# A graph layer and 64 routed experts on one core: the beginning in another order

## The chip, the core and the metric

The kernel runs on one core of a Trainium2 chip. The metric is the device time of one execution in microseconds (us). TensorE multiplies, VectorE, ScalarE and GpSimd compute elementwise, and SyncE only issues DMAs in the kernel before. Each engine works through its own program in order, and semaphores tie them together.

## The reference, cut to what matters

```python
# x: 1024 nodes x 512;  16384 edges (src, dst, edge_weight), sorted by dst
def gnn(H, W, bias, edge_row, edge_col, edge_val):
    HW = H @ W
    msgs = edge_val[:, None] * HW[edge_col]
    out = segment_sum(msgs, edge_row, num_segments=1024)
    return relu(out + bias)

x = x + gnn(layernorm(x), W, bias, src, dst, edge_weight)
# 64 experts, 2 per token, hidden 256, plus one small shared expert
n = layernorm(x)
x = x + sum over the token's two experts e of w_e * ffn_e(layernorm(n)) + shared(layernorm(n))
```

The change lies wholly in the first part: the weighted adjacency matrix A (1024 x 1024, built from the edge list) and HW = layernorm(x) @ W. What follows (messages A @ HW, routing, experts) is computed as before.

## The kernel before, in words

**Adjacency.** The 16384 edges make 128 tiles of 128 edges. For a tile, ScalarE builds a one-hot matrix `osl` (line 587, eight tiles at a time, then one Relu at line 590), and VectorE and GpSimd build weighted one-hots `M` (lines 835 and 459; the buffers are named `M` and `AT` in rows, since two of four lie in the tile AT). Four tiles are a quad. TensorE multiplies them into one of four PSUM banks (line 1129), and VectorE adds that bank into A (`sums`, lines 803 to 812: clear the bank that was added before, line 811; add, line 812). The program has 32 quads. VectorE's adds run three quads behind its `M` tiles (`BEHIND`). In each quad GpSimd makes one `M` tile and VectorE three. `osl` has two buffers, each for two quads, so ScalarE may build the next only when TensorE has used the buffer.

**x.** The rows of x are 8 blocks of 128. A block's way is: mean and variance (VectorE, lines 736 to 745), inverse deviation (GpSimd, line 430), the standardised rows `xh` (VectorE, line 821), four transposes (TensorE, line 1117), a copy to `xhT` (ScalarE, line 594), the product with W (TensorE, line 1136), a copy to HW (ScalarE, line 599). In the rows fp32 matmuls are counted twice: a quad is 8 of them, a product is 8.

**The order.** TensorE goes through four pairs of blocks (`pair`). For each block it does: transposes of the block, four quads, the product. In what follows *a block* is this unit: four quads with one block of x. At the start come the edge arithmetic on VectorE (lines 749 to 797), which ends in `edges_ready`, and transposes of small weights on TensorE (lines 1097 and 1105, `raw`). SyncE issues all loads, the last being x blocks 2 to 7 and W (lines 306 and 307), then a fill of the DRAM tensor `slots` (`sentinel`), then the weights of the first four expert pairs. ScalarE clears all of A (line 579). GpSimd scales the small shared weights (lines 470 and 471: `R` and `Wsb`) after its first pair.

After the last product TensorE waits for all adds (line 1148), transposes A (line 1156) and goes on with the messages.

Of the kernel before, what the change touches and what calls it, by code (L numbers as in the profile page):

```python
# [21 lines left out]
POOL_M = 1  # L22
# [13 lines left out]
def moe_gnn(nc, x, src, dst, ew, W, bias, Wg, bg, gamma, beta, W1, b1, W3, b3, W2, b2,  # L36
# [18 lines left out]
    with ctx:  # L55
# [58 lines left out]
        sentinel = HW[:, 0:5, :].rearrange("p b d -> p (b d)")[:, 0:(EXPERTS * LIST + P) * REC // P]  # L114
# [172 lines left out]
        def _(sp):  # L287
# [5 lines left out]
            v3 = "e (c d) -> e c d"  # L293
            for to, a in ((raw_wg, Wg), (raw_g, gamma), (raw_b, beta)):
                sp.dma_start(to, a.rearrange(v3, c=4)).then_inc(raw_in, 16)
            sp.dma_start(raw_b13[:, 0:2, :], b1.rearrange(v3, c=HC)).then_inc(raw_in, 16)
            sp.dma_start(raw_b13[:, 2:4, :], b3.rearrange(v3, c=HC)).then_inc(raw_in, 16)
            sp.dma_start(gs4[:, 0, :], gs.rearrange("(p c) -> p c", c=DC)).then_inc(small_in, 16)
            sp.dma_start(gs4[:, 1, :], bs.rearrange("(p c) -> p c", c=DC)).then_inc(small_in, 16)
# [3 lines left out]
            sp.dma_start(Ws[:, :, 0:32], Ws1.rearrange("(p c) n -> p c n", c=DC)).then_inc(ws_in, 16)  # L303
            sp.dma_start(Ws[:, :, 32:64], Ws3.rearrange("(p c) n -> p c n", c=DC)).then_inc(ws_in, 16)
            for i in range(1, 4):
                sp.dma_start(X[:, 2 * i:2 * i + 2, :], xv[:, 2 * i:2 * i + 2, :]).then_inc(x_in[i], 16)
            sp.dma_start(GW[:, :, :], W.rearrange("(p c) n -> p c n", c=DC)).then_inc(gw_in, 16)

            sp.wait_ge(consts, 6)
# [12 lines left out]
            for v in range(RING // 2):  # L322
                load_up(v, v)
                load_down(v, v)
# [81 lines left out]
        def _(pool):  # L406
# [10 lines left out]
            g.memset(sentinel, NOWHERE).then_inc(consts, 1)  # L417
# [4 lines left out]
                   allow_small_or_imprecise_dtypes=True).then_inc(consts, 1)  # L422
            pool_n = [0]
# [13 lines left out]
            inverse_deviations(range(0, 2), 1)  # L437
            pool.wait_ge(edges_ready, 1)
            R1 = pool.value_load(rounds_sb[0:1, 0:1], min_val=1, max_val=N // WIN)

            def pair(r, j, first):

                half = (r * (NB // 2) + j) * 4
                for h in range(4):
# [6 lines left out]
                    for q in (2 * h, 2 * h + 1):  # L451
                        if not first or q >= 4:
                            pool.wait_ge(quad_done[q % 2], half + (q // 2 - 1))
                        elif q == 2:
                            pool.wait_ge(raw_transposed, 2)
                        hold(pool)
                        for k in range(POOL_M):
# [6 lines left out]
            inverse_deviations(range(2, NB), 2)  # L464

            pool.wait_ge(small_in, 80)
            pool.wait_ge(ws_in, 32)
            pool.wait_ge(raw_transposed, 2)
            for c in range(DC):
                g.tensor_scalar(R[:, c, 64:128], Ws[:, c, :], gs4[:, 0, c:c + 1], None, ALU.mult)  # L470
                ins = g.tensor_scalar(Wsb[:, c, :], Ws[:, c, :], gs4[:, 1, c:c + 1], None, ALU.mult)
            ins.then_inc(wsb_ready, 1)
# [104 lines left out]
        def _(act):  # L577
            a = nc.scalar
            a.memzero(A[:, :]).then_inc(a_chain, 4)
# [12 lines left out]
            def x_transposed(g, u):  # L592
                act.wait_ge(xhT_ps, g + 1)
                a.copy(xhT[:, u, :, :].rearrange("p c n -> p (c n)"), bank[4 + u][:, :]).then_inc(xhT_ready, 1)

            def x_times_w(g, u):
                act.wait_ge(hw_ps, g + 1)
                act.wait_ge(sentinel_out, 16)
# [789 lines left out]
```

## Time and profile before

| | |
|---|---|
| times of three runs | 458.48, 459.57, 460.67 us; median 459.57 |
| the profiled execution | 458.82 us, its span 457.1 us |
| TensorE busy | 391.7 us (86%) |
| VectorE, ScalarE, GpSimd busy | 207.7, 166.1, 154.9 us |
| moved by DMA | 126.11 MB, 276 GB/s on average |

The first fifth of the span (to 85.5 us) is the part with A and HW; from there to about 160 us come the messages and the routing, then a short serial part, and from about 190 us the experts. The chain of waits ends with TensorE for 81% of the span.

### The profile page before, as it was taken

Reading aid. Unit: us, or ns where it says so; the run is one execution under the profiler, and the core shown is the slowest. Engines: PE = TensorE matmul, PEld = TensorE weight load, DVE = VectorE, ACT = ScalarE, POOL = GpSimd, SP = SyncE. Lnnn points to the kernel's source line nnn. Section 1 sums busy time; section 2 is a strip of 40 time slices with the busy share of each in tenths; the row PEclk is TensorE's granted clock in tenths of the full one; section 3 lists DMA queues with packets and bytes.
Section 4 is the critical chain, followed back from the end, with each engine's and each line's share of the span. In section 5 each row is a group of like instructions: output and inputs, shape, how many; then the busy total and the mean of one; then the engine's idle time right before and its main releaser. Section 6 shows DMA issues by size and latency. Waiting matters only on the chain.

```text
span 457.1 us, 6545 instructions
## 1 busy us (share of the span) xinstructions
PE 391.7 (86%) x1811; PEld 202.3 (44%) x1812; DVE 207.7 (45%) x685; ACT 166.1 (36%) x414; POOL 154.9 (34%) x262
## 2 busy tenths in 40 slices
PE   2699999999999987999999999986988979888600
PEld 1586767656565553344344443433434433343100
DVE  5889888216666586532333233313113123222036
ACT  9859999223223220233233323331213231131200
POOL 2575553014654657232333223323113122110000
PEclk9989999999999995899999999999889898898855
DMA  4999600100004545499999999999999999996068
GB/s 113 328 383 408 276 0 0 42 25 24 24 25 122 222 156 197 144 389 408 404 408 407 405 408 409 407 406 408 407 406 409 406 405 404 403 405 271 20 250 303
DMA packets 41779, 126.11 MB, mean 276 GB/s; under 512 B 7953, under 2 KB 8529, under 8 KB 41618
## 3 DMA queue, kind: packets, MB, share of 16 engines
q1 hardware_dynamic: 35954, 117.29, 66.3%
q0 software_dynamic: 5792, 8.43, 5.3%
q8 instruction: 14, 0.23, 0.2%
q14 instruction: 19, 0.16, 0.1%
HBM read 121.22 MB, written 13.39 MB: 294 GB/s over the span
## 4 chain that ended last, share of the span: by engine, by line
PE 81%; issue 5%; DMA 5%; DVE 3%; SPq 3%; POOL 1%; ACT 1%; ACTq 0%; DVEq 0%; POOLq 0%
PE bank L1295 29%; PE bank L1312 13%; PE bank L1168 12%; PE bank L1129 6%; PE bank L1136 6%; PE bank L1304 5%; PE bank L1288 4%; DMA w<-totals 2%; DMA X<-in_x_dram 2%; PE bank L1156 2%; PE bank L1187 1%; PE bank L1236 1%; PE bank L1177 1%; PE bank L1117 1%; SPq L398 1%
## 5 line engine op out<-in xcount | busy, mean ns | idle before, releaser
L1031 DVE SCALAR_TENSOR_TENSOR osl<-bank,b13T,osl 128x64 f32<-128x64 f32 x132 | 28.4, 277 | 171.5 <-ACT osl L675 171.5
L1295 PE MATMUL bank<-w,xhT 128*64 128x512 f32 x368 | 91.9, 645 | 14.7 <-issue 14.5
L668 ACT COPY xh<-bank 128x512 f32<-128x512 f32 x33 | 19.3, 585 | 149.0 <-PE bank L1295 149.0
L1168 PE MATMUL bank<-HW,AT 128*128 128x512 f32 x128 | 58.2, 592 | 0.0
L1295 PEld LDWEIGHTS bank<-w,xhT 128*64 128x64 f32 x368 | 28.6, 147 | 61.5 <-issue 60.1
L545 POOL DMA_INDIRECT totals<-osl,A x17 | 17.0, 1000 | 91.5 <-PE bank L1288 72.1
L1312 PE MATMUL bank<-w,osl 128*64 128x512 f32 x184 | 45.0, 608 | 3.2 <-DVE osl L1031 3.2
L545 POOL DMA_INDIRECT totals<-GW,A x16 | 16.0, 999 | 87.2 <-PE bank L1288 71.6
L587 ACT ACTIVATE osl<-iota,eT 128x128 f32<-128x128 f32 x128 | 39.0, 389 | 6.1 <-PE bank L1129 6.1
L541 POOL DMA_INDIRECT A<-nx_rows,A x33 | 34.4, 1041 | 10.5 <-issue 10.5
L1168 PEld LDWEIGHTS bank<-HW,AT 128*128 128x128 f32 x128 | 22.9, 191 | 21.0 <-issue 21.0
L675 ACT ACTIVATE osl<-bank,b13T 128x64 f32<-128x64 f32 x132 | 30.7, 314 | 4.0 <-issue 1.0
L1304 PEld LDWEIGHTS bank<-ident,xh 128*128 128x128 f32 x132 | 18.3, 208 | 26.6 <-issue 26.0
L1136 PE MATMUL bank<-GW,xhT 128*128 128x512 f32 x64 | 28.8, 592 | 0.0
L1312 PEld LDWEIGHTS bank<-w,osl 128*64 128x64 f32 x184 | 14.5, 140 | 28.6 <-issue 28.6
L1304 PE MATMUL bank<-ident,xh 128*128 128x128 f32 x132 | 24.6, 309 | 0.5 <-ACT xh L668 0.5
L1129 PE MATMUL bank<-AT,osl 128*128 128x128 f32 x128 | 19.3, 302 | 4.6 <-DVE AT L835 3.7
L1014 DVE TENSOR_TENSOR xhT<-xhT,bT 128x512 f32<-128x512 f32 x32 | 22.2, 692 | 1.1
L1288 PE MATMUL bank<-ident,A 128*128 128x128 f32 x132 | 22.3, 293 | 0.0
L1295 PE MATMUL bank<-A,xhT 128*64 128x512 f32 x80 | 20.0, 644 | 2.3 <-issue 2.3
L1013 DVE TENSOR_TENSOR xhT<-bank,gT 128x512 f32<-128x512 f32 x32 | 21.8, 681 | 0.2 <-issue 0.2
L1295 PE MATMUL bank<-HW,xhT 128*64 128x512 f32 x80 | 20.0, 644 | 2.0 <-issue 1.9
(208 smaller groups left out, 543.2 us busy)
## 6 DMA issues: line engine op xcount, KB each, us to landing
w<-in_L_ffn_W_dram SPq DMA_DIRECT2D x66, 1024.0 KB
A<-in_L_ffn_W_dram SPq DMA_DIRECT2D x15, 1024.0 KB
HW<-in_L_ffn_W_dram SPq DMA_DIRECT2D x10, 1024.0 KB
AT<-in_L_ffn_W_dram SPq DMA_DIRECT2D x5, 1024.0 KB
w<-totals SPq DMA_DIRECT2D x8, 512.0 KB, 7.5
w<-in_L_ffn_W_dram SPq DMA_DIRECT2D x6, 512.0 KB
X<-in_x_dram SPq DMA_DIRECT2D x4, 512.0 KB, 7.2
out_dram<-X SPq DMA_DIRECT2D x8, 256.0 KB, 5.7
```

The source lines that it names most:

```text
L541: g.indirect_dma_start(xg[b], None, nx_rows, bass.IndirectOffsetOnAxis(ap=index, axis=0), bounds_check=N - 1, oob_is_err=False).then_inc(x ...
L545: g.indirect_dma_start(totals, bass.IndirectOffsetOnAxis(ap=index, axis=0), ysb[b], None, bounds_check=2 * N - 1, oob_is_err=False).then_i ...
L587: ins = a.activation(osl[:, h % 2, k, :], iota[:, :], ACT.Abs, bias=eT[:, 1, ds(j * 32 + 8 * h + k, 1)])
L675: ins = a.activation(sl[b][:, m, CAP * h:CAP * h + CAP], bank[4][:, m * P + CAP * h:m * P + CAP * h + CAP], ACT.Silu, bias=b13T[:, 0, m, c ...
L1031: ins = v.scalar_tensor_tensor(hT[b][:, m, CAP * h:CAP * h + CAP], bank[4][:, (HC + m) * P + CAP * h:(HC + m) * P + CAP * h + CAP], b13T[: ...
L1129: ins = t.matmul(bank[q % 4][:, ds(at[k], TW)], osl[:, (q // 2) % 2, (q % 2) * QUAD + k, :], Mq[q % 4][:, k, :], start=False, stop=(k == Q ...
L1136: ins = t.matmul(bank[6 + u][:, :], xhT[:, u, c, :], GW[:, c, :], start=(c == 0), stop=(c == DC - 1))
L1168: ins = t.matmul(bank[4 + s % 2][:, :], AT[:, s % 2, k, :], HW[:, k, :], start=(k == 0), stop=(k == NB - 1))
L1288: ins = t.transpose(bank[b][:, c * P:(c + 1) * P], xg[i][:, c:c + DC * (P - 1) + 1:DC], ident[:, :])
L1295: ins = t.matmul(bank[2 + b][CAP * h:CAP * h + CAP, :], xe[b][:, c, CAP * h:CAP * h + CAP], up_w[v][:, h, :, c, :], start=(c == 0), stop=( ...
L1304: ins = t.transpose(bank[4][:, i * P:(i + 1) * P], hraw[b][:, at:at + HC * (P - 1) + 1:HC], ident[:, :])
L1312: ins = t.matmul(bank[6 + b][CAP * h:CAP * h + CAP, :], hT[b][:, m, CAP * h:CAP * h + CAP], down_w[v][:, h, m, :], start=(m == 0), stop=(m ...
```

## The change

Loads: after the edge arrays and x blocks 0 and 1, SyncE now issues W and the other x blocks. The small weights are issued from ScalarE's queue ahead of everything else on it. A is cleared in three parts: columns 0 to 2599 by VectorE, to 5399 by GpSimd, the other 2920 by ScalarE. The `sentinel` values lie in an expert weight buffer instead of HW, and SyncE waits for their transfer before it loads the fourth pair's weights.

Order: a block's product now stands ahead of its quads, and the transposes of the next block stand between the two. VectorE standardises block 0 in the middle of the edge arithmetic and copies `xhT` (ScalarE copies the first one only). The statistics of x blocks 2 to 7 stand in three parts between the quads of the second block. GpSimd makes two `M` tiles in each odd quad, except in the first four quads, and scales the shared weights ahead of its first tile. ScalarE waits for that (`wsb_ready`) ahead of its second group of one-hots.

```diff
+A_DVE, A_POOL = 2600, 5400
+def pool_tiles(q, first):
+    return 2 if q % 2 and not (first and q < 4) else 1
 # sync
             sp.dma_start(X[:, 0:2, :], xv[:, 0:2, :]).then_inc(x_in[0], 16)
+            sp.dma_start(GW[:, :, :], W.rearrange("(p c) n -> p c n", c=DC)).then_inc(gw_in, 16)
+            for i in range(1, 4):
+                sp.dma_start(X[:, 2 * i:2 * i + 2, :], xv[:, 2 * i:2 * i + 2, :]).then_inc(x_in[i], 16)
...
             for v in range(RING // 2):
+                if v == RING // 2 - 1:
+                    sp.wait_ge(sentinel_out, 16)
                 load_up(v, v)
 # gpsimd
+            g.memset(A[:, A_DVE:A_POOL], 0.0).then_inc(a_chain, 1)
+            g.memset(sentinel, NOWHERE).then_inc(consts, 1)
             inverse_deviations(range(0, 2), 1)
+            pool.wait_ge(ws_in, 64)
+            pool.wait_ge(raw_transposed, 2)
+            for c in range(DC):
+                g.tensor_scalar(R[:, c, 64:128], Ws[:, c, :], gs4[:, 0, c:c + 1], None, ALU.mult)
+                ins = g.tensor_scalar(Wsb[:, c, :], Ws[:, c, :], gs4[:, 1, c:c + 1], None, ALU.mult)
+            ins.then_inc(wsb_ready, 1)
...
+                        if first and q in (5, 7):
+                            b = q - 3
+                            inverse_deviations(range(b, b + 2), b // 2 + 1)
 # scalar
-            a.memzero(A[:, :]).then_inc(a_chain, 4)
+            for to, of in ((raw_wg, Wg), (raw_g, gamma), (raw_b, beta)):
+                act.dma_start(to, of.rearrange(v3, c=4)).then_inc(raw_in, 16)
... six more loads
+            a.memzero(A[:, A_POOL:]).then_inc(a_chain, 1)
-            def pair(j, last):
+            def pair(j, first, last):
                 half = j * 4
-                x_transposed(j * 2, 0)
-                one_hots(half, j, 2, False)
-                one_hots(half, j, 3, False)
-                x_times_w(j * 2, 0)
-                x_transposed(j * 2 + 1, 1)
+                for u in range(2):
+                    if u:
+                        one_hots(half, j, 2, False)
+                    one_hots(half, j, 2 * u + 1, first)
+                    x_times_w(j * 2 + u, u)
                 if not last:
                     one_hots(half + 4, j + 1, 0, False)
-                    one_hots(half + 4, j + 1, 1, False)
-                    x_times_w(j * 2 + 1, 1)
 # vector
+            v.memset(A[:, 0:A_DVE], 0.0).then_inc(a_chain, 2)
...
+            def transposed_rows(b, u):
+                dve.wait_ge(xhT_ps, b + 1)
+                if not isinstance(b, int) or b > 1:
+                    dve.wait_ge(hw_ps, b - 1)
+                v.tensor_copy(xhT[:, u, :, :]..., bank[4 + u][:, :]).then_inc(xhT_ready, 1)
... in sum_pair, for each q
+                    if with_x and q % 4 == 3 and not (last and u):
+                        transposed_rows(b + 1, 1 - u)
+                    if with_x and first and q in (3, 4, 6):
+                        c = {3: 2, 4: 4, 6: 6}[q]
+                        mean_and_variance(range(c, c + 2))
+                    if with_x and first and q in (5, 6):
+                        dve.wait_ge(rstd_ready, 2)
+                        standard_rows(q - 3, q - 5)
+                    if with_x and not first and not last and q % 4 == 1:
+                        dve.wait_ge(rstd_ready, 4)
+                        dve.wait_ge(xhT_ps, b + 1)
+                        standard_rows(b + 2, u)
 # tensor
                 for u in range(2):
-                    if with_x:
-                        ... (transposes of this block)
+                    if with_x and not (first and u == 0):
+                        x_product(j * 2 + u, u)
+                        if not (last and u):
+                            x_rows(j * 2 + u + 1, 1 - u)
                     for q in range(4 * u, 4 * u + 4):
...
-                    if with_x:
-                        ... (product of this block)
```

On TensorE, the program from the product for the edge table to the first quad before (line 1117 is a block's transposes, the first M rows a quad):

```order
L1090 MATMUL bank<-wrow,ones 128x128
L1097 MATMUL bank<-ident,AT 128x64 x12
L1105 MATMUL bank<-ident,AT 128x64 x4
L1108 TENSOR_LOAD rounds_sb
L1108 ISA x2
L1139 UNCONDITIONAL_BRANCH
L1139 ISA
L1117 MATMUL bank<-ident,xh 128x128 x4
```

The same stretch now (line 1139 is transposes, line 1149 a product with W, line 1154 the product for the edge table, line 1172 the first quad's offsets):

```order
L1125 MATMUL bank<-ident,AT 128x64 x12
L1133 MATMUL bank<-ident,AT 128x64 x4
L1139 MATMUL bank<-ident,xh 128x128 x4
L1154 MATMUL bank<-wrow,ones 128x128
L1149 MATMUL bank<-GW,xhT 128x512 x4
L1139 MATMUL bank<-ident,xh 128x128 x4
L1159 TENSOR_LOAD rounds_sb
L1159 ISA x2
L1172 TENSOR_LOAD wrow
```

The small weights, the transposes of blocks 0 and 1 and the first product now stand ahead of the first quad.

On VectorE, the first quads' tiles before (line 821 is `xh`, 835 the `M` tiles, 741 and 744 the statistics of six x blocks, 812 the first add):

```order
L821 TENSOR_SCALAR xh<-X,mv,rstd 128x512
L826 MEMSET bank 128x384 x2
L835 TENSOR_SCALAR M<-iota,eT 128x128 x3
L821 TENSOR_SCALAR xh<-X,mv,rstd 128x512
L835 TENSOR_SCALAR M<-iota,eT 128x128 x3
L741 BN_STATS stats<-X 128x6 x6
L744 BN_AGGR mv<-stats 128x2 x6
L830 MEMSET bank 128x384 x2
L835 TENSOR_SCALAR AT<-iota,eT 128x128 x6
```

And now, from the same tiles to the tiles of the second block's second quad (line 854 `M` tiles, 828 an add, 835 the copy to `xhT`, 748 and 751 statistics of two x blocks):

```order
L854 TENSOR_SCALAR M<-iota,eT 128x128 x6
L849 MEMSET bank 128x384 x2
L854 TENSOR_SCALAR AT<-iota,eT 128x128 x6
...
L828 TENSOR_TENSOR A<-A,bank 128x384
L835 COPY xhT<-bank 128x512
L748 BN_STATS stats<-X 128x6 x2
L751 BN_AGGR mv<-stats 128x2 x2
L854 TENSOR_SCALAR M<-iota,eT 128x128 x3
...
L828 TENSOR_TENSOR A<-A,bank 128x384
L748 BN_STATS stats<-X 128x6 x2
L751 BN_AGGR mv<-stats 128x2 x2
```

The statistics have moved from between the first block's tiles to between the second block's, in three parts.

## Rows read from the trace of the kernel before

**Rows 1.** Busy time by stretch, in us from the span's start.

```profile
core 0: us, PE busy (x) PEld busy (x) DVE busy (x) ACT busy (x) POOL busy (x), PEclk, DMA share, GB/s
22.66:26.10 3.44, 3.44 (x16) 3.44 (x17) 3.36 (x12) 0.03 (x1) 0.83 (x1) 0.50 0.99 314
37.71:85.50 47.79, 46.88 (x263) 33.77 (x262) 38.80 (x117) 41.33 (x105) 20.07 (x38) 1.00 0.34 135
85.50:160.00 74.50, 74.50 (x306) 43.89 (x305) 38.62 (x169) 21.25 (x43) 34.51 (x85) 1.00 0.22 74
191.00:411.00 220.00, 202.95 (x962) 86.63 (x960) 65.86 (x188) 63.67 (x184) 59.17 (x58) 0.96 1.03 406
```

**Rows 2.** Chain of waits, the beginning: start, duration (us), what.

```profile
10.30 7.58 DMA X<-in_x_dram
...
22.66 3.67 PE bank L1129 x16
26.33 3.44 PE bank L1136 x8
...
30.23 3.57 PE bank L1129 x32
```

**Rows 3.** Chain of waits, a block and the end of the part.

```profile
62.19 2.73 PE bank L1129 x24
64.96 1.15 PE bank L1129 x8
...
69.55 0.47 PE bank L1117 x4
...
85.50 0.88 PE bank L1156 x8
```

**Rows 4.** Timeline of the beginning: start, duration, engine, line, what.

```profile
2.07 7.14 ACT L579 ACTIVATE A<-A 128x8320 uint32<-128x8320 uint32 x1
...
9.12 2.43 ACT L587 ACTIVATE osl<-iota,eT 128x128 f32<-128x128 f32 x8
...
11.54 0.29 DVE L797 TENSOR_TENSOR eT<-eT,bank 128x128 f32<-128x128 f32 x1 [0.20 <-PE bank L1090]
...
12.78 0.57 DVE L821 TENSOR_SCALAR xh<-X,mv,rstd 128x512 f32<-128x512 f32 x1 [0.94 <-DVE eT L797]
...
15.22 3.78 PE L1129 MATMUL bank<-M,osl 128*128 128x128 f32 x16 [0.64 <-POOL M L459]
...
16.54 3.94 DVE L741 BATCH_NORM_STATS2 stats<-X 128x6 f32<-128x512 f32 x6 [0.39 <-DMA X<-in_x_dram]
...
21.80 1.44 DVE L835 TENSOR_SCALAR AT<-iota,eT 128x128 f32<-128x128 f32 x6
```

**Rows 5.** SyncE's issue of a small load, from the timeline.

```profile
2.64 0.57 SPq L295 DMA_DIRECT2D AT<-in_L_ffn_Wg_dram  x1
```

**Rows 6.** DMA issues: count, KB each, median us to landing.

```profile
GW<-in_L_gnn_W_dram SPq DMA_DIRECT2D x1, 1024.0 KB, 10.0
...
HW<-in_L_ffn_Ws_dram SPq DMA_DIRECT2D x2, 64.0 KB, 5.7
```

**Rows 7.** Timeline of ScalarE and TensorE in the repeating blocks.

```profile
38.09 1.06 ACT L590 ACTIVATE osl<-osl 128x1024 f32<-128x1024 f32 x1
...
39.52 0.59 ACT L594 COPY xhT<-bank 128x512 f32<-128x512 f32 x1
...
39.97 2.35 PE L1129 MATMUL bank<-AT,osl 128*128 128x128 f32 x16 [0.47 <-POOL M L459]
...
48.18 2.45 ACT L587 ACTIVATE osl<-iota,eT 128x128 f32<-128x128 f32 x8 [0.26 <-PE bank L1129]
```

**Rows 8.** Timeline of VectorE: a copy out of PSUM, then adds in the repeating blocks.

```profile
8.02 0.54 DVE L767 COPY eT<-bank 128x384 f32<-128x384 f32 x1
...
39.16 0.38 DVE L811 MEMSET bank<- 128x384 f32 x1
...
40.84 0.38 DVE L811 MEMSET bank<- 128x384 f32 x1
```

**Rows 9.** GpSimd, its instructions of one line: duration in ns, lowest, median, highest.

```profile
L459 POOL TENSOR_SCALAR AT<-iota,small x12: 790/793/1124, 35.6 to 74.5; 128x128 f32<-128x128 f32 x12
...
L470 POOL TENSOR_SCALAR R<-HW,gs x4: 437/439/541, 29.2 to 31.8; 128x64 f32<-128x64 f32 x4
```

**Rows 10.** Timeline of VectorE: the last add into A.

```profile
82.76 0.54 DVE L812 TENSOR_TENSOR A<-A,bank 128x384 f32 x1
```

More of the change, by code:

```diff
@@ L832, in sum_pair @@
                         dve.wait_ge(raw_transposed, 2)
-                    for k in range(POOL_M, QUAD):
+                    for k in range(pool_tiles(q, with_x and first), QUAD):
                         t = j * 32 + (QUAD * q + k)
@@ L837, in sum_pair @@
                     ins.then_inc(m_ready, 1)
-                    if with_x and first and q == 1:
-                        mean_and_variance(range(2, NB))
                     if q >= BEHIND:
@@ L1088, in _ @@
             t.matmul(bank[1][0:1, P:2 * P], mx, ident[:, :], start=True, stop=True).then_inc(edges_transposed, 1)
-            pe.wait_ge(base_ready, 1)
-            t.matmul(bank[1][:, 384:512], ones[0:1, :], neg_base, start=True, stop=True).then_inc(base_ps, 1)
             pe.wait_ge(raw_in, 80)
@@ L1106, in _, with x_rows, x_product, pair @@
             ins.then_inc(raw_transposed, 1)
+            def x_rows(g, u):
+                pe.wait_ge(xh_ready, g + 1)
+                for c in range(DC):
+                    ins = t.transpose(bank[4 + u][:, c * P:(c + 1) * P], xh[:, u, c:c + DC * (P - 1) + 1:DC], ident[:, :])
+                ins.then_inc(xhT_ps, 1)
+            def x_product(g, u):
+                pe.wait_ge(gw_in, 16)
+                pe.wait_ge(xhT_ready, g + 1)
+                if not isinstance(g, int) or g > 1:
+                    pe.wait_ge(hw_ready, g - 1)
+                for c in range(DC):
+                    ins = t.matmul(bank[6 + u][:, :], xhT[:, u, c, :], GW[:, c, :], start=(c == 0), stop=(c == DC - 1))
+                ins.then_inc(hw_ps, 1)
+            x_rows(0, 0)
+            pe.wait_ge(base_ready, 1)
+            t.matmul(bank[1][:, 384:512], ones[0:1, :], neg_base, start=True, stop=True).then_inc(base_ps, 1)
+            x_product(0, 0)
+            x_rows(1, 1)
             pe.wait_ge(edges_ready, 1)
             R1 = pe.value_load(rounds_sb[0:1, 0:1], min_val=1, max_val=N // WIN)
-            def pair(r, j, with_x):
+            def pair(r, j, with_x, first=False, last=False):
                 half = pe.snap((r * (NB // 2) + j) * 4)
@@ L1131, in pair @@
                         ins.then_inc(quad_done[q % 2], 1)
-                    if with_x:
-                        pe.wait_ge(gw_in, 16)
-                        pe.wait_ge(xhT_ready, j * 2 + u + 1)
-                        for c in range(DC):
-                            ins = t.matmul(bank[6 + u][:, :], xhT[:, u, c, :], GW[:, c, :], start=(c == 0), stop=(c == DC - 1))
-                        ins.then_inc(hw_ps, 1)
-            with pe.Fori(0, NB // 2) as j:
+            pair(0, 0, True, first=True)
+            with pe.Fori(1, NB // 2 - 1) as j:
                 pair(0, j, True)
+            pair(0, NB // 2 - 1, True, last=True)
             with pe.If(R1 > 1):
```

87 lines of the change are left out of this document (36 added, 51 removed).

## The prediction

> **What bounds the kernel now.** I read the busy time by stretch first, then the chain of waits, then the timeline where the chain leaves TensorE. By stretch [rows 1] TensorE is busy for 46.88 of the 47.79 us from 37.71 to 85.50, and for all of the 74.5 us behind it. So what this part saves should move the end, if nothing later absorbs it. The experts run from 191 with the DMA at 406 GB/s, its share at the top: they are paced by loads. But each of these loads waits for a product of the experts' own (`h_ps`), so the stream of loads begins earlier when the experts do. I therefore carry a gain at 85.5 to the end in full. The chain at the beginning [rows 2] runs through the load of x that lands at 17.88, then the late start of TensorE's second half block at 22.66. The timeline [rows 4] tells why: VectorE does the statistics of six x blocks from 16.54 to 20.48 ahead of the tiles `AT` at 21.80, so TensorE, done at 19.00, stands still for 3.66 us. In the repeating blocks the chain is TensorE's alone [rows 3], but its pace is not free: three quads take 2.73 us (0.91 each) and the last 1.15.
>
> The pace tells a second thing. The first 16 quad matmuls took 3.78 us, the next 16 took 3.67, and later 32 took 3.57 [rows 2, 4]. For the second sixteen the granted clock was 0.50, the lower level of 1.2 GHz [rows 1]; the first sixteen had the same pace. TensorE had stood still before, and once it had worked for 3.4 us the product behind it went at full pace (3.44 us, as everywhere). The Trainium skill's page "TensorE: Matmul & The Clock Gate", Part 1, says that the throttled clock is the default and that work releases it; the trace agrees by those two paces. A start with less standing still saves twice, but a first product placed earlier can fall into the slow stretch.
>
> **Part 1, the beginning.** I compare the moment at which TensorE has done the quads and products of two blocks and the transposes of the third: before, 30.23 + 3.57 + 3.44 + 0.47 = 37.71 [rows 2, 3].
>
> The edge table was ready at 11.83 [rows 4]. VectorE's standardised rows of block 0 now stand ahead of it: +0.57, so 12.4; with 0.1 for crowded loads 12.5. ScalarE first issues nine loads; at SyncE's 0.57 to 0.6 each [rows 5] that is 5.4 us from 0.8, then its table (1.3 us, the stretch to 2.07 before) and 2920/8320 of 7.14 = 2.5 us of clearing: free at 10.0 instead of 9.21. Its one-hots end at 12.45 and the copy of the transposed block 0 at 13.0. The product can start at 13.1. W was 10.0 us in landing behind everything else [rows 6]; issued at 2.6 it is here by 12.6 even at that, so it costs nothing. TensorE has had only short work till then, so I take the slow clock for 3.4 us: that does 1.7 of the product's 3.44, the rest takes 1.7, then 0.47 for transposes: 18.7, and the first quad runs 19.0 to 19.9.
>
> VectorE meanwhile has made tiles of all four quads (12.5, then 0.95 as from 11.83 to 12.78, rows 0.57, two clearings 0.76, tiles 1.44, clearings 0.76, tiles 1.44: 18.4), so it no longer delays block 0. From the first quad's end it is the bound. It adds (20.0 to 20.6); copies the transposed block 1 (0.54 for 384 columns [rows 8], so 0.7 for 512: 21.3); and then does block 1's quads. A quad with three tiles takes 40.84 - 39.16 = 1.68 [rows 8]; one with two takes 0.24 less (1.44 for six tiles [rows 4]) = 1.44. Statistics for two x blocks: 3.94 for six plus the aggregates, 1.5 for two. So: statistics 22.8, quad 4 24.5, statistics 26.0, quad 5 27.4, rows of block 2 28.0, quad 6 29.7, statistics 31.2, rows of block 3 31.8, tiles and cleared bank of quad 7 32.7, its add of quad 4 and the copy of block 2 33.9. TensorE's product of block 1 and quads hide under this; quad 7 ends at 33.6. The compared moment comes at 33.8: a gain of 3.9.
>
> What hides the statistics is thus gone in block 1: 4.5 us of them, 1.4 of copies and 1.1 of rows lie on the path there, instead of one stall and a cold clock in block 0.
>
> **Part 2, the repeating blocks.** Six remain, with five sets of transposes before as now: before, (47.79 + 0.47)/6 = 8.04 us each. TensorE's own work is 3.57 + 3.44 + 0.47 = 7.48. ScalarE loses two copies of 0.59 per pair [rows 7], but it cannot run ahead: a one-hot buffer is free only when its two quads are done. From a block's quads at 0: the first buffer is free at 1.82, ScalarE starts 0.15 later, and two groups take 2 x (2.45 + 1.06) less small overlaps = 6.97 [rows 7], so the second group for the next block is ready at 8.94, or 8.94 - P after that block's quads begin, for a period P. TensorE needs another 0.82 from there to its first matmul (38.09 + 1.06 = 39.15 to 39.97 [rows 7]) and then runs the two quads in 2.1 to 2.3. So P = (9.76 - P) + 2.1 + 3.91, P = 7.88. The stretch takes 6 x 7.88 - 0.47 = 46.8 instead of 47.8, a gain of 1.0, and quads end at 80.6. Its bounds are 7.48 and 8.04 a block. VectorE per block has 2 x 1.68 + 2 x 1.44 + 0.57 + 0.7 + waits 0.2 = 7.7, GpSimd 6 tiles of 0.79 and its small copies, about 6 [rows 9]: both just fit.
>
> **Part 3, the end of the part.** Before, VectorE's last adds lay under the last product: quads ended at 82.06, the last add at 83.30 [rows 10]. That cover is gone, since quads now come last. So TensorE waits 1.24 us plus 0.15 to wake: A's transposes start at 82.0 instead of 85.50 [rows 3]. Of that part the bounds are 1.1 (one clearing and add) and 2.2 (two quads' adds behind).
>
> **At nothing.** VectorE's 2600 columns at 0.38 per 384 [rows 8] are 2.6 us, before the edge arrays are used; GpSimd's clearing and sentinel end some 2 us before it is needed. If either overran, at most 1 us. The wait for the sentinel holds only loads not used for 190 us. Earlier expert weights change nothing. GpSimd's eight scalings, 8 x 0.44 = 3.5 [rows 9], need the shared weights: issued by 5.6 and 5.7 in landing they are there at 11.3, so GpSimd is free at 14.8, in time for tiles wanted at 19.
>
> The sum: 3.9 + 1.0 - 1.4 = 3.5, which is 85.50 - 82.0. The profiled execution took 458.82, so 455.3; it lay 0.75 under the median of the runs. From the median, 459.57 - 3.5 = 456.1. I say 456.0.
>
> The Trainium skill speaks against one half of the edit: "DMA: Bandwidth & Descriptors", section "Issuing engines are not separate DMA queues", says loads issued from two engines run on the same 16 DMA engines and only issue time is saved. By it W and x land earlier because they are issued earlier and not because there are two queues. No row before shows two queues at once; the sum above goes by the order of issue alone.
>
> **The rivals.**
>
> *Clock low for longer.* If the first product goes wholly at the lower clock (+1.7), or TensorE's gaps in block 1 (2 us before the transposes of block 2, 1 before quad 7) bring the clock down again (half of 3.4 us: +1.7), the gain is 1.8, or 0.1 with both: 457.8 to 459.5. For it: the stop of 3.66 us before did it [rows 1]. Against: these stops are shorter.
>
> *Small loads late.* If the shared weights take W's 10.0 us instead of 5.7 [rows 6], they are there at 15.6, GpSimd is free at 19.1, ScalarE's second one-hots end at 22.6, and the third quad starts at 23.4 instead of 20.8. VectorE's own chain hangs on the first quad, which GpSimd's tile delays by 0.8 to 1.5. Time 457.5.
>
> *Better than summed.* If the clock is up before the first product (-1.7) and blocks take 7.6 (-1.7), the gain is 6.9: 452.7. For it: these are the lower bounds of both terms. Against: the same slow pace at 15.22 after four us of small transposes.
>
> *VectorE becomes the bound: slower.* Its 7.7 us per block rests on instructions that overlap. GpSimd gets 12 tiles a pair instead of 8. If tiles of the two hold each other up, as the highest 1124 ns of a tile at 793 suggests [rows 9], each of a block's 16 tiles could cost 0.1 more and the copy wait besides: 9.3. It decides from 7.88 + (3.5 + 2.3)/6 = 8.85 on; at 9.2 the six blocks cost 8 us more than forecast and the time is 464. Against: VectorE is idle for 9.0 of 47.79 us [rows 1], and only 0.2 us a block is added net (6.24 + 0.57 + 0.7 for 4 x 1.68 + 0.57). The Trainium skill's page "SBUF — State Buffer", "Who interferes with whom", says a VectorE instruction in a two-port mode and GpSimd lock each other out wholly. By that rule this rival gains; no row here separates it.
>
> **How the numbers follow.** Forecast 0.45 (its own range 454.7 to 457.3), clock low 0.25, small loads late 0.1, better 0.13, VectorE bound 0.07. The measurement tells a change from none at about 0.5%, or 2.3 us. Faster: nearly all of the forecast, the better case, a fifth of the two small-gain cases: 0.62. Slower 0.07, same 0.31. Range 452.8 to 459.2: it leaves out the rival on the slow side and part of the double clock loss and of the better case.
>
> **What would show it.** First quad near 19; statistics between 21 and 31 on the chain; no wait for the x load; blocks of 7.9 us; TensorE idle 1.4 us before A's transposes at about 82; the experts as long as before. A first quad after 21, blocks over 8, or a GpSimd tile on the chain would make it wrong.

## The result and the profile after

The kernel became slower: 464.5 us (median of 4 runs, 462.49 to 466.38) against 459.02 (458.41 to 460.67) for the kernel before on the same chip. The ratio is 1.012, with a 95% interval of 1.0084 to 1.0157. The forecast was 456.0. The profiled execution took 463.57 us, its span 461.8.

First the busy time by stretch of the changed kernel (columns as in [rows 1]), for the first quads, the six repeating blocks, the stretch from A's transposes on, and the experts:

```profile
core 0: us, PE busy (x) PEld busy (x) DVE busy (x) ACT busy (x) POOL busy (x), PEclk, DMA share, GB/s
25.06:28.43 3.37, 3.37 (x16) 3.37 (x17) 0.73 (x2) 2.69 (x6) 3.03 (x8) 0.50 1.03 412
41.25:88.80 47.55, 45.90 (x261) 33.29 (x259) 41.63 (x120) 41.30 (x106) 33.29 (x58) 1.00 0.17 68
90.46:164.96 74.50, 74.50 (x305) 43.98 (x306) 38.61 (x169) 20.76 (x42) 34.39 (x85) 1.00 0.22 74
195.96:415.96 220.00, 203.31 (x962) 86.89 (x960) 65.80 (x188) 63.73 (x184) 59.17 (x58) 0.96 1.03 406
```

The last two rows are those of before within 0.5 us [rows 1]. From A's transposes to the span's end it is 371.3 us, before 371.6. So the whole loss lies ahead of A's transposes, which begin at 90.46 instead of 85.50, and nothing behind them absorbs or adds anything.

The chain of waits, beginning (start, duration, what):

```profile
3.32 7.74 DMA AT<-in_L_ffn_b_dram
...
21.20 0.48 POOL R L442
...
24.12 0.82 POOL M L467
25.06 2.09 PE bank L1179 x8
```

The reader is to see two names that the chain of before had not [rows 2]: a load of small weights at the start, and GpSimd's scalings (`R`, lines 442 and 443) ahead of the first `M` tile. TensorE's timeline of the same stretch:

```profile
11.11 1.73 PE L1125 MATMUL bank<-ident,AT 64*128 64x64 f32 x12 [2.84 <-DMA AT<-in_L_ffn_b_dram]
...
14.30 0.79 PE L1154 MATMUL bank<-wrow,ones 1*128 1x128 f32 x2
15.14 6.57 PE L1149 MATMUL bank<-GW,xhT 128*128 128x512 f32 x8
21.55 0.63 PE L1139 MATMUL bank<-ident,xh 128*128 128x128 f32 x4
25.06 3.78 PE L1179 MATMUL bank<-M,osl 128*128 128x128 f32 x16 [2.88 <-POOL M L467]
```

And what the other engines waited for (GpSimd, ScalarE, VectorE):

```profile
20.20 0.55 POOL L442 TENSOR_SCALAR R<-HW,gs 128x64 f32<-128x64 f32 x1 [9.36 <-DMA gs<-in_L_ffn_bs_dram]
...
14.41 0.58 ACT L621 COPY xhT<-bank 128x512 f32<-128x512 f32 x1
...
23.77 2.44 ACT L596 ACTIVATE osl<-iota,eT 128x128 f32<-128x128 f32 x8 [6.74 <-POOL AT L443]
...
15.23 0.29 DVE L813 TENSOR_TENSOR eT<-eT,bank 128x128 f32<-128x128 f32 x1 [1.53 <-PE bank L1154]
...
27.70 0.56 DVE L828 TENSOR_TENSOR A<-A,bank 128x384 f32 x1 [6.24 <-PE bank L1179]
```

GpSimd stood still for 9.36 us until a load of 2 KB was there; ScalarE waited behind it for 6.74, then TensorE and VectorE. The row at 14.41 is the copy of the transposed block 0, which the first product reads. The loads themselves (KB each, median us from issue to landing):

```profile
AT<-in_L_ffn_b_dram ACTq DMA_DIRECT2D x2, 64.0 KB, 6.8
HW<-in_L_ffn_Ws_dram ACTq DMA_DIRECT2D x2, 64.0 KB, 10.1
...
gs<-in_L_ffn_gs_dram ACTq DMA_DIRECT2D x1, 2.0 KB, 10.1
gs<-in_L_ffn_bs_dram ACTq DMA_DIRECT2D x1, 2.0 KB, 12.9
```

The last 2 KB were issued at 7.21 and landed 12.9 us later, at 20.1. W itself took 8.5, less than the 10.0 of before [rows 6].

The end of the part is as forecast in kind:

```profile
90.46 1.13 PE L1201 MATMUL bank<-ident,A 128*128 128x128 f32 x8 [1.43 <-DVE A L828]
```

### The profile page after: what moved, and what is told of

Read it like the earlier page. It is cut to its first block, busy times and chain, and to the rows that moved or that the text cites. A ratio compares the mean times of both kernels' runs of the same rounds, so it can differ in the third digit from the quotient of the medians.

```text
span 461.8 us, 6407 instructions
## 1 busy us (share of the span) xinstructions
PE 395.0 (86%) x1811; PEld 203.6 (44%) x1812; DVE 210.3 (46%) x679; ACT 158.0 (34%) x407; POOL 170.0 (37%) x281
## 4 chain that ended last, share of the span: by engine, by line
PE 73%; issue 9%; DVE 7%; DMA 5%; DVEq 1%; POOL 1%; ACTq 1%; ACT 1%; SPq 1%; POOLq 0%
PE bank L1340 28%; PE bank L1357 13%; PE bank L1213 12%; PE bank L1349 5%; PE bank L1333 4%; DMA w<-totals 2%; PE bank L1179 2%; PE bank L1149 2%; DMA AT<-in_L_ffn_b_dram 2%; DVE A L828 2%; PE bank L1201 2%; PE bank L1232 1%; PE bank L1281 1%; DVE bank L827 1%; PE bank L1222 1%
## 5 line engine op out<-in xcount | busy, mean ns | idle before, releaser
L596 ACT ACTIVATE osl<-iota,eT 128x128 f32<-128x128 f32 x120 | 36.6, 387 | 13.5 <-POOL AT L443 6.7
L1149 PE MATMUL bank<-GW,xhT 128*128 128x512 f32 x64 | 31.9, 645 | 0.0
L467 POOL TENSOR_SCALAR M<-iota,small 128x128 f32<-128x128 f32 x23 | 19.0, 834 | 8.8 <-PE bank L1179 7.6
L1333 PE MATMUL bank<-ident,A 128*128 128x128 f32 x132 | 22.2, 293 | 0.0
```

What stands on the lines that cost most here:

```text
L596: ins = a.activation(osl[:, h % 2, k, :], iota[:, :], ACT.Abs, bias=eT[:, 1, ds(j * 32 + 8 * h + k, 1)])
L1149: ins = t.matmul(bank[6 + u][:, :], xhT[:, u, c, :], GW[:, c, :], start=(c == 0), stop=(c == DC - 1))
L1333: ins = t.transpose(bank[b][:, c * P:(c + 1) * P], xg[i][:, c:c + DC * (P - 1) + 1:DC], ident[:, :])
```

## The experiments

Times are compared with the kernel before on the same chip. That kernel's median was 458.37 us beside e1 to e4, 459.15 beside e5 to e8 and 459.45 beside e9 and e10. A difference in us is a difference of ratios times 459. Beside it stands where A's transposes begin in the profiled execution (before 85.50, changed kernel 90.46).

| kernel | median us | ratio (95%) | A's transposes |
|---|---|---|---|
| changed kernel | 464.5 | 1.012 (1.0084 to 1.0157) | 90.46 |
| e1 scalings back | 461.05 | 1.0045 (1.0024 to 1.0066) | 87.14 |
| e2 shared weights issued first | 462.69 | 1.0097 (1.0067 to 1.0126) | 88.12 |
| e3 last product last | 466.27 | 1.0182 (1.0159 to 1.0204) | 90.96 |
| e4 before + loads, clearing | 460.92 | 1.0063 (1.0042 to 1.0085) | 86.68 |
| e5 four one-hot buffers | 459.56 | 1.0001 (0.9973 to 1.0029) | 86.53 |
| e6 before + four buffers | 457.33 | 0.9950 (0.9921 to 0.9978) | 83.58 |
| e7 one queue, e1, e5 | 455.89 | 0.9931 (0.9907 to 0.9955) | 81.78 |
| e8 e7 + last product last | 456.22 | 0.9948 (0.9923 to 0.9972) | 84.01 |
| e9 e7 with two buffers | 458.19 | 0.9983 (0.9956 to 1.0011) | 83.27 |
| e10 e7, scalings first | 454.47 | 0.9886 (0.9849 to 0.9924) | 82.86 |

### The scalings back behind the first pair

```diff
 # gpsimd, ahead of its first tile
-            pool.wait_ge(ws_in, 64)
-            ... (eight scalings)
+                        elif q == 2:
+                            pool.wait_ge(raw_transposed, 2)
...
             pair(0, 0, True)
+            pool.wait_ge(ws_in, 64)
+            ... (eight scalings)
 # scalar: the wait for wsb_ready moves from its first pair to its last copy of HW
```

> The changed kernel, with GpSimd's eight scalings of the shared weights put back behind its first pair, and ScalarE's wait for them put back ahead of the last copy to HW. Theory L (the first quad waits for small loads: the last 2 KB load lands at about 20.1, the eight scalings take 3.5, GpSimd's first tile is ready at 24.9, the first quad at 25.06): GpSimd makes its first tile before 20, the first quad moves to the end of block 1's transposes, 22.2, plus the offset load, so 22.3 to 22.8; the part ends about 2.3 us earlier, A's transposes near 88.2, time about 2.3 under the changed kernel. Rival V (VectorE's statistics in block 1 set the pace whatever the first quad does): the first quad moves and A's transposes stay within 0.7 of 90.46. Rival C (the clock: the first quads come sooner behind the product, so they run at the full pace): 3.6 us for four quads instead of 6.8, another 1 to 1.5 us gained, so 3.5 to 4 in all.

Ratio 1.0045, and TensorE's timeline:

```profile
21.32 1.95 PE L1182 MATMUL bank<-M,osl 128*128 128x128 f32 x16
23.10 1.95 PE L1182 MATMUL bank<-AT,osl 128*128 128x128 f32 x16
...
36.32 3.65 PE L1152 MATMUL bank<-GW,xhT 128*128 128x512 f32 x8
...
41.63 1.15 PE L1182 MATMUL bank<-M,osl 128*128 128x128 f32 x8 [0.30 <-POOL M L463]
43.10 1.15 PE L1182 MATMUL bank<-AT,osl 128*128 128x128 f32 x8 [0.32 <-POOL AT L463]
44.81 0.37 PE L1182 MATMUL bank<-AT,osl 128*128 128x128 f32 x1 [0.56 <-POOL AT L463]
```

The first quads no longer wait and run at full pace (1.95 us where it was 3.78). The third product begins at 36.32 instead of 41.09, so the scalings' wait, with the stop and the slow quads behind it, costs 4.8 us there. Of that 3.3 arrive at A's transposes (3.4 by the ratios): the scalings now cost 1.18 us in the third block (the three POOL waits), and the end has a longer stop (2.14 us for 1.43). That is the gain of the third case of the expectation, in which the first quads also run at full pace; the first case had 2.3. The wait is the largest single cause, but without it the kernel is still slower than before.

### The shared weights issued first

```diff
 # scalar, its own queue
+            ... (Ws1, Ws3, gs, bs)
             ... (raw_wg, raw_g, raw_b, raw_b13)
-            ... (Ws1, Ws3, gs, bs)
```

> The changed kernel, with ScalarE's queue issuing the four smallest loads (shared weights and their two scale vectors) ahead of the five raw weight loads. Theory L: they are issued by 3.5 instead of 8.2 and land by 9 to 10, so GpSimd starts its scalings when the raw transposes are done, at 13.3 to 14.5, and is through before 18; the first quad at 22.3 to 22.8, as with the scalings moved; the raw weights land up to 1 us later than 11.06, which moves the first product by as much. Time 1.5 to 2.5 under the changed kernel. Rival Q (the queue from ScalarE is slow by itself, whatever the order): the two 2 KB loads take over 8 us again, gain under 1.

Ratio 1.0097. The 2 KB of `bs` now landed in 3.6 us and the wait was gone, but the weights that TensorE transposes took 6.7 to 7.6 and came late:

```profile
13.59 1.72 PE L1125 MATMUL bank<-ident,AT 64*128 64x64 f32 x12 [5.31 <-DMA AT<-in_L_ffn_b_dram]
...
17.62 5.62 PE L1149 MATMUL bank<-GW,xhT 128*128 128x512 f32 x8
...
23.54 1.95 PE L1179 MATMUL bank<-M,osl 128*128 128x128 f32 x16
```

The first quad is at 23.54, where 22.3 to 22.8 was expected. By the ratios the gain over the changed kernel is 1.1 us, under the 1.5 to 2.5 expected, and the two intervals overlap, so it is not shown by the times. Within the small queue the order only picks who is late. Both kinds of small weights stand ahead of the first quad, one on TensorE, one on GpSimd.

### The last product behind the last quads

```diff
 # tensor
-                    if with_x and not (first and u == 0):
+                    if with_x and not (first and u == 0) and not (last and u):
                         x_product(j * 2 + u, u)
...
+                    if with_x and last and u:
+                        x_product(j * 2 + u, u)
```

> The changed kernel, with the last block's product behind its quads, as before the change, all else as changed. Theory T (the end of the part lost its cover: TensorE stood still 1.43 us at 89.0 for VectorE's last adds): A's transposes follow the last product without a stop, at 89.0 to 89.2, and the time is 1.3 to 1.4 less than that of the changed kernel. Rival: ScalarE's one-hots for the last two quads, which the chain showed late by 0.62, come relatively later with the product gone from in front (it covered them), so the last quads wait up to 1.8 more and nothing is won or 1 us is lost.

Ratio 1.0182: slower still. The idle time moved and grew:

```profile
82.13 2.11 PE L1179 MATMUL bank<-M,osl 128*128 128x128 f32 x16 [2.44 <-ACT osl L599]
85.53 2.16 PE L1179 MATMUL bank<-AT,osl 128*128 128x128 f32 x16 [1.29 <-DVE bank L827]
87.52 3.60 PE L1149 MATMUL bank<-GW,xhT 128*128 128x512 f32 x8
90.96 1.04 PE L1203 MATMUL bank<-ident,A 128*128 128x128 f32 x8
```

The 1.43 us ahead of A are gone, but the last quads now come a product sooner, and wait 2.44 and 1.29 us. The profile names one-hots for the first wait and a cleared bank for the second; the one-hots were done at 81.47 and 84.90, about 0.65 us ahead of the quads both times, so the second wait may be for them too. A product between two blocks' quads is the cover under which ScalarE builds; the lost cover at the end can't be had back this way.

### Only the loads and the clearing

```diff
 # the kernel before, with its order and its statistics
+ the loads on two queues and A cleared by three engines, as in the changed kernel
```

> The kernel before, with only the start of the change: x and W first on SyncE's queue, the small weights on ScalarE's, A cleared by three engines, the sentinel values in the weight buffer. Order of the work as before. Theory L (the crowded loads cost by themselves: edge arrays land 1.1 later, x block 0 1.9 later, raw weights at 11.06): the edge table is ready at about 14.7 instead of 11.83, the first quad near 18 instead of 15.22; x blocks 2 to 7 are there before their statistics, which gives back 0.4 of idle VectorE, so the part ends 1.5 to 2.5 later than before: time 460.5 to 461.5. Rival: the earlier x and W pay for it (statistics not waiting, W there early), no change against before, within 0.5.

Ratio 1.0063. The edge table came at 13.29 (before 11.83) and the first quad at 16.44 (before 15.22), both earlier than the 14.7 and 18 expected, and A's transposes 1.18 us later. The ratio's 2.9 us are more than that; the one profiled execution was the fastest of the four (459.90). So this part alone costs, and gains nothing in the order of before: the stop for the statistics is still there (second half block at 23.21, 3.00 idle).

### Four one-hot buffers

The free expert weight buffers of the start hold two more groups of `osl`, so ScalarE may run a whole block ahead. The load of expert weights into their place moves behind `edges_ready`, in all kernels with four buffers.

```diff
-                if not first or h >= 2:
-                    act.wait_ge(quad_done[1], half + (h - 1))
+                if not isinstance(half, int) or half + h > 3:
+                    act.wait_ge(quad_done[1], half + (h - 3))
-                            a.activation(osl[:, h % 2, k, :], ...
+                            a.activation(oslb[h % 4][:, k, :], ...
```

In the changed kernel:

> The changed kernel with four one-hot buffers instead of two (the third and fourth lie in the last expert weight buffer, whose load moves behind the adjacency part). Theory S (blocks alternate between 7.5 and 8.5 us because ScalarE may start a group only when TensorE has used the buffer: the sum of two blocks is fixed at about 2.0 + 6.97 + 0.82 + 2.3 + 3.91 = 16.0): ScalarE can work through, so blocks take TensorE's own 7.48 to 7.6, six blocks 45.0 to 45.6 instead of 47.65, and the gain over the changed kernel is 2 to 2.6. Rival V (VectorE with 7.5 to 7.7 us a block is the bound): blocks 7.7 to 7.9, gain 0.5 to 1.5. Rival Q (the offset loads of TensorE's own program set the pace, 1.15 a quad): no gain.

Ratio 1.0001, so 5.5 us better than the changed kernel by ratio. TensorE's first quads and its blocks:

```profile
25.21 2.14 PE L1183 MATMUL bank<-M,osl 128*128 128x128 f32 x16 [3.33 <-POOL M L471]
...
40.32 3.65 PE L1153 MATMUL bank<-GW,xhT 128*128 128x512 f32 x8
...
47.85 3.60 PE L1153 MATMUL bank<-GW,xhT 128*128 128x512 f32 x8
...
55.32 3.60 PE L1153 MATMUL bank<-GW,xhT 128*128 128x512 f32 x8
...
86.53 1.11 PE L1205 MATMUL bank<-ident,A 128*128 128x128 f32 x8 [1.60 <-DVE A L832]
```

A block takes 7.48 us, TensorE's own work and nothing else. In the changed kernel products began at 41.09, 48.62, 57.22, 64.80, 73.28 and 80.76: 7.5 and 8.5 or 8.6 in turn. A long block, with its wait:

```profile
54.92 2.40 PE L1179 MATMUL bank<-AT,osl 128*128 128x128 f32 x16 [0.45 <-POOL M L467]
57.22 3.70 PE L1149 MATMUL bank<-GW,xhT 128*128 128x512 f32 x8
```

The profile names a tile of GpSimd as what ended this wait. But these quads read `AT` tiles, which GpSimd had done at 52.76; the `M` tile it names is for the quads behind. ScalarE's one-hots for them were done at 54.10, 0.82 us ahead, the same 0.82 as before the change [rows 7]. The four buffers, which change only how early ScalarE may start, take the wait away, so it was for the one-hots.

The profile accounts for 3.9 us (90.46 to 86.53) of the 5.5; the rest is not located.

In the kernel before:

> The kernel before with the same four one-hot buffers. Theory S says that there ScalarE's own work, 4 x 3.45 + 4 x 0.47 = 15.7 us a pair, takes over at once, so a pair falls from 15.98 to 15.7 only and the kernel gains 0.5 to 1. Rival: if the buffers alone were the bound in both, it gains as much as the changed kernel does, 2 to 2.6.

Ratio 0.995. A's transposes begin at 83.58, 1.92 earlier. Its blocks take 7.48 to 7.84, since the quads of a second half still take 2.24 to 2.31 where the full pace is 1.95. The beginning is as before (first quad 15.13 for 15.22), so the gain is in the blocks and not in the load that moved. ScalarE's first pair is unrolled here too. With buffers to spare the changed order is thus worth up to 0.36 us a block over the order of before; with two buffers it is worth nothing.

### One queue, the scalings back, four buffers

```diff
 # sync
             ... (edges, x blocks 0 and 1)
+            ... (raw_wg, raw_g, raw_b, raw_b13)
             sp.dma_start(GW ...)
             ... (x blocks 2 to 7)
+            ... (Ws1, Ws3, gs, bs), then the three to bc
 # scalar: issues no loads
```

> The changed kernel with three things: all loads from SyncE's queue again, in the order edges, x blocks 0 and 1, raw weights, W, the other x, the smallest last; the scalings behind the first pair; four one-hot buffers. Theory L (two queues at once delay exactly what is waited for first): raw weights land near 8.6 as before the change, the edge table is ready at 13.2 to 13.6, the first product starts near 13 and the first quad near 19; A's transposes start at 80.5 to 82, time 453.5 to 456. Rival Q (crowding is by bytes, W and x behind the raw weights slow them whatever the queue): raw weights at 10.5 or later and the first quad at 21, time 456 to 458.

Ratio 0.9931, better than both kernels.

```profile
8.90 1.73 PE L1132 MATMUL bank<-ident,AT 64*128 64x64 f32 x12 [0.64 <-DMA AT<-in_L_ffn_b_dram]
...
12.93 5.38 PE L1156 MATMUL bank<-GW,xhT 128*128 128x512 f32 x8
18.15 0.64 PE L1146 MATMUL bank<-ident,xh 128*128 128x128 f32 x4
18.62 1.95 PE L1186 MATMUL bank<-M,osl 128*128 128x128 f32 x16
```

The first quad at 18.62 and A's transposes at 81.78 are where the forecast had put them (19.0 and 82.0). For A's transposes that is partly luck: the forecast had two buffers and 7.88 us a block. Here the third block took 9.47 and the others TensorE's 7.48; the third is long since the scalings hold up GpSimd's tiles there. The interval overlaps that of e6, so this run doesn't show that the other changes add anything to four buffers. The same with the last product last:

> The kernel of the run before it with the last block's product behind its quads. Theory T2 (in the earlier run the product's move failed because ScalarE's one-hots, held by two buffers, had lost their cover; four buffers give it back): TensorE has no stop of 1.4 at the end of the part and the gain over that kernel is 1.0 to 1.4. Rival V: VectorE's tiles for the last quads are late as well (1.29 in that run), so it gains 0 to 0.5.

Ratio 0.9948, the interval over that of e7. Even with four buffers the last quads waited 0.64 and 1.10 us, both until 0.6 us after ScalarE's one-hots were done (74.42 and 77.84), and the first quad began at 19.84 in this execution: no gain is shown.

### One queue with two buffers, and the scalings in a covered place

The first is e7 with the two buffers of the changed kernel. The second is e7 with the scalings ahead of GpSimd's first tile again, and `Ws1`, `Ws3`, `gs`, `bs` issued right behind W.

> The changed kernel with all loads issued by SyncE in one row (edges, x blocks 0 and 1, the small weights that TensorE transposes, W, x, the shared weights, the smallest last) and GpSimd's eight scalings behind its first pair; two one-hot buffers as in the changed kernel, where the run before had four. Theory that loads and buffers add up: the beginning is that of the run with four buffers (edge table at 13.3, first quad near 18.6, the third product near 33.8), that is 2.7 us ahead of the run with only the scalings moved (21.3); the six repeating blocks then alternate 7.5 and 8.5 us, 3.1 more in all than with four buffers. TensorE begins to transpose A at 84.5, the ratio to the kernel before is 0.997 to 1.000. Rival, the queue gives nothing that the buffers did not give: first quad still after 21, A at 87, ratio 1.0045.

Ratio 0.9983, as by the first theory, though A's transposes began at 83.27 and not at 84.5. Its rival (1.0045, as e1) lies outside the interval. First quad at 18.45; the third block took 9.47 us with the scalings, then 7.48 and 8.5 to 8.1 in turn. So one queue in the order of need against two is worth 2.8 us (0.9983 against 1.0045 of e1), and the buffers 2.4 more (e7). The interval of e9 holds 1: with two buffers the changed order, its loads in time, is not shown to be faster than the kernel before.

> One queue and four one-hot buffers as in the run at 455.9 us, but the shared weights are issued right behind W and ahead of x blocks 2 to 7, and GpSimd scales them ahead of its first tile, where the changed kernel put them; GpSimd waits 4.8 us there for the edge table anyway. Theory, the scalings cost nothing where the weights are there in time: landed by 11.5, scaled by 15.1, first quad at 18.6 to 19.0, and the GpSimd waits of the third block (0.29, 0.32, 0.56) are gone. TensorE begins to transpose A at 80.6 to 81.0, 1 us ahead of the earlier run, ratio 0.990 to 0.992. Rival: the smallest loads land late here too (6.3 us from issue for 2 KB, as in the earlier run), so at 14.4; scalings end at 18, GpSimd's first tile at 19, the first quad at 20 and A at 82: ratio 0.993 to 0.995.

Ratio 0.9886, the best version. The timeline (GpSimd, then TensorE):

```profile
13.98 0.46 POOL L455 TENSOR_SCALAR R<-HW,gs 128x64 f32<-128x64 f32 x1 [3.41 <-DMA gs<-in_L_ffn_bs_dram]
...
18.10 1.73 POOL L480 TENSOR_SCALAR M<-iota,small 128x128 f32<-128x128 f32 x2
...
14.61 6.73 PE L1153 MATMUL bank<-GW,xhT 128*128 128x512 f32 x8
21.18 0.63 PE L1143 MATMUL bank<-ident,xh 128*128 128x128 f32 x4
21.65 1.95 PE L1183 MATMUL bank<-M,osl 128*128 128x128 f32 x16
...
40.61 1.95 PE L1183 MATMUL bank<-M,osl 128*128 128x128 f32 x16
```

The rival was right that the 2 KB land late (13.98), the theory that the scalings then cost nothing: they lie under the first product, and the third block has no wait for GpSimd. But A's transposes began at 82.86, later than either had said, as the small weights and the first product were late in this execution. That A begins 1.1 us later than in e7 while the ratio is lower may be the choice of execution: the profiled one was the slowest of e10's six, 1.8 us above their median, and that of e7 was 1.0 below its own. The two intervals overlap, so that e10 beats e7 is not shown. That it beats both original kernels is.

## Why the prediction was wrong

**Where the step failed.** The forecast had A's transposes at 82.0, they began at 90.46: 8.5 us late. In parts: the first quad 6.1 (25.06 for 19.0), from there to the third product 1.4 (16.2 for 14.8), the six blocks 0.85 (47.65 for 46.8), the end 0.15. The step that failed is the one put "at nothing": "issued by 5.6 and 5.7 in landing they are there at 11.3, so GpSimd is free at 14.8". The last of these loads was issued at 7.21 (1.6 later) and took 12.9 us (7.2 more), so they were there at 20.1 and GpSimd was free at 23.7. By the ratios, e1 without that wait is 3.4 us faster, and one queue in the order of need 2.8 more (e9). That leaves 458.2 against the 456.0 said.

**The first quad.** In the changed kernel it is GpSimd's wait alone that sets it. The first products of e3 and e5, whose first loads and order are the same, took 5.4 and 6.0 us to the next transposes and not 6.4, and their first quads still stood at 24.68 and 25.21, behind stops of 3.60 and 3.33 us. Without the wait the first quad is at 21.32 (e1), 2.3 later than forecast. So two smaller misses lay hidden under the large one.

The first of them is the start of the first product: 15.14, 2.0 after the forecast's 13.1. Two chains end there together. ScalarE's nine loads took it up to 8.2, not 6.2 as the 0.57 to 0.6 each had given, so its one-hots end at 14.49 for 12.45, and its copy of block 0 at 14.99 for 13.0. And the transposes that it copies stood behind those of the small weights, which waited for their load until 11.11; they end at 14.37. In e2 ScalarE was free and stood 4.07 us for these transposes: there the load alone puts the first product at 17.62. e7 takes away both, and its product begins at 12.93.

The second of them is the length of that product: 6.4 us to the next transposes instead of 5.1. It is not the change's own: between executions of the changed kernel and its variants it was 5.2 to 6.6.

The edge table was late too: ready at 15.52 for 12.5. VectorE could begin the statistics at 8.12 only, when x was there (6.22 before; 0.1 was allowed for it), and on TensorE the product for the table stood behind the same transposes. The rows of the program showed that order ahead of the prediction, but its working let the edge table wait for VectorE alone. It cost nothing here: VectorE's tiles of the first block were done at 21.46, ahead of the end of TensorE's transposes at 22.2.

**Block 1.** 1.4 us over the forecast. VectorE sets this block's pace, and its first add, which waits for the first quad, came 2.64 us after that quad's begin, where 1.0 was forecast. It was 1.61 in e1 and 1.72 to 1.75 in e5 and e3. The first sixteen matmuls of the changed kernel took 3.78 us at the lower clock (0.50 in the first row above). From that add on the third product came 13.4 us later in all four, against 13.8 forecast, so VectorE's chain of statistics, adds and rows was right. What set the clock is less sure: it was down behind the stop of 2.88 here, and fell 1.0 us after the stop of 3.60 in e3, but a stop of 3.33 in e5 left it at 1.00.

The rival "clock low for longer" came true in its first half, nearly (6.4 us of at most 6.8). Its second half did not come as written: in block 1's own gaps the clock stayed at 1.00, and it was down at block 0's quads, behind a stop that belongs to "small loads late". In e10 it did fall behind such a gap (2.11 us, then 0.50) and cost nothing: the third product came 15.0 us after the first quad, as in e1, where it stayed up. "Small loads late" I had given 0.10 and priced at loads landing by 15.6. The two rivals were not independent, and each price was a bound taken from uncrowded rows.

**The blocks.** The mechanism (ScalarE can't run ahead, a buffer comes free only when its quads are done) was right; its size was not. The two terms that were short: "runs the two quads in 2.1 to 2.3", entered as 2.1, was 2.30 the first time and 2.15 the second (54.92 to 57.22, 71.13 to 73.28); and these quads began 9.87 and 9.91 us after the quads of the block ahead, not 9.76. Two blocks took 16.1 us, as 7.5 or 7.6 and 8.5 or 8.6, where 15.8 was forecast and 16.0 was before. So Part 2's gain of 1.0 was nothing. e5 shows the mechanism: with four buffers ScalarE no longer waits and a block is 7.48. VectorE and GpSimd fit, as forecast, even then. The rival in which VectorE becomes the bound fell: the six blocks took 47.65 us, and VectorE was busy for 41.63 of 47.55. GpSimd's tiles did get longer (median 898 ns for half of them, 793 before [rows 9]); in e5 that costs nothing, and in the changed kernel no wait is shown to come of it.

**The end.** 1.4 forecast, 1.43 measured. That step was right. e3 tried to have it back and lost more, and e8 gained nothing that shows.

**Loads.** The Trainium skill, "DMA: Bandwidth & Descriptors", section "Issuing engines are not separate DMA queues", says that a second issuing engine saves only the issue time. The runs agree and are harsher: the second queue put small weights beside the 1 MB loads of the other, and one queue in order of need was 2.8 us faster (e9 against e1). Three things differ between these two: the number of queues, W issued behind the small weights instead of ahead of them, and ScalarE free of issuing. No run separates them; two queues with W held back was not tried. The prediction cited the rule, then costed the small loads by their landing time of before, when little lay beside them.

**What is left open.** The 5.5 us of the measured ratio are 5.0 at A's transposes; the rest is within the interval. Elsewhere the ratio and the begin of A's transposes differ by up to 2.9 us. One execution of each kernel is profiled: that of e3 was the fastest of its four (1.8 under their median), that of e10 the slowest of its six. From A's transposes to the span's end the profiled executions lie between 368.0 and 374.2 us (371.6 before). The three at 368 (e5, e6, e9) are the fastest or next to fastest of their kernels, 3.3 to 5.2 us under the median, so this is more likely a spread between executions than a gain of these kernels. In e1 and e2 some 1.5 us of it are the lower clock right behind the stop ahead of A, as these rows of e1 show:

```profile
86.00:88.00 2.00, 0.86 (x5) 0.89 (x6) 0.00 (x0) 0.00 (x0) 0.00 (x0) 0.86 0.04 12
88.00:90.00 2.00, 2.00 (x12) 2.00 (x11) 0.00 (x0) 1.17 (x2) 0.00 (x0) 0.50 0.01 4
```

The stop was 2.14 us in e1 and 1.58 in e2; one of 1.60 in e7 left the clock at full. What tells these apart, and what makes an execution end in 368 us, wasn't tried.

## What to carry to other kernels

Before you move work ahead of the first use of an engine, list every load and every instruction that then stands in front of it on each queue, and price the loads by rows in which as much was in flight. Issue in the order of need on one queue: here small loads on a second queue weren't ahead of the big ones but among them. Where two engines hand work to and fro through two buffers, work out that loop's period before you move anything else, and try more buffers first: here the loop set the pace and the order of the rest didn't. Four buffers alone gave 0.5% to the kernel before.

## What the runs showed of the hardware

- A 2 KB load took 12.9 us to land when it was the last of nine on ScalarE's queue beside 3 MB of x and W and the first expert weights on SyncE's; 2.4 us in the kernel before, 3.6 when issued among the first, 4.1 to 6.3 as one of the last in one queue.
- Issues from ScalarE's queue took 0.57 to 1.34 us each with SyncE issuing too (up to 1.48 in e1); the same loads took SyncE alone 0.43 to 0.63 in the kernel before. One queue doesn't guard against it: with W and x issued ahead of it, one of the 2 KB loads took SyncE 2.54 us to issue in e7.
- The granted clock reads 1.00 from the span's start, but the first product ran at half pace under it: weight loads of 0.34 us and 0.81 to 0.85 from one to the next, then 0.19 and 0.43 (e7, TensorE's weight loads):

```profile
14.77 0.34 PEld L1156 LDWEIGHTS bank<-GW,xhT 128*128 128x128 f32 x1 [0.52 <-issue]
15.62 0.34 PEld L1156 LDWEIGHTS bank<-GW,xhT 128*128 128x128 f32 x1 [0.52 <-issue]
16.43 0.19 PEld L1156 LDWEIGHTS bank<-GW,xhT 128*128 128x128 f32 x1 [0.47 <-issue]
```

  In the changed kernel six weight loads of this product have 0.34 us, and its row reads 1.00 too. Ahead of the first fall that the profile records, the pace tells the clock and the row doesn't.
- Four kernels with all loads on SyncE (e7 to e10) had the small weights ready for TensorE at 8.90, 10.09, 8.40 and 10.59: with e7 and e8, whose beginnings are the same, 1.2 us apart. One profile can't place a beginning more closely than that.
- With the same beginning up to the first quad, a stop of TensorE of 3.33 us left the granted clock at 1.00 (e5), and stops of 2.88 (changed kernel) and 3.60 (e3) were followed by 0.50.
